# One more pass through TensorE's loop ahead of tile 0, and tile 0 turned and split by its own row blocks

## The reference

```
logits = z @ router_w + router_b            # 8 experts
top1   = argmax(softmax(logits))
h      = z @ w1[e] + b1[e]                  # 256 -> 2 x 1024
a, g   = split(h, 2)
y      = (a * sigmoid(g)) @ w2[e] + b2[e]   # 1024 -> 256, for the tokens with top1 == e
out    = x + y
```

## Time and profile before

| | us |
|---|---|
| median of 3 runs | 236.19 (235.63, 236.19, 237.41) |
| profiled execution | 235.62 |
| its span | 233.8 |
| TensorE busy in the span | 208.6 (89%) |
| DVE, ACT, POOL busy | 162.4, 123.8, 124.4 |
| mean granted TensorE clock | 0.947 of full |

### The profile page before, as it was taken

One profiled execution on the slowest core, in us unless ns is written; L12 is line 12 of the kernel. 1 busy time (PEld: TensorE's weight loads), 2 busy tenths in 40 slices (PEclk: granted clock), 3 DMA queues, 4 the chain that ended last, 5 costly groups with the idle time before them and its releaser, 6 DMA issues.

```text
span 233.8 us, 4272 instructions
## 1 busy us (share of the span) xinstructions
PE 208.6 (89%) x1505; PEld 196.2 (84%) x1507; DVE 162.4 (69%) x306; ACT 123.8 (53%) x204; POOL 124.4 (53%) x148
## 2 busy tenths in 40 slices
PE   7989858994799999999999999999999999999800
PEld 3858317994799999999999999999999999999700
DVE  5759935765902799389979969956995699559300
ACT  2457902453702858286785776738672757375000
POOL 5000177860800387438878778774877177018133
PEclk9999975999589999999999999999999999999985
DMA  5996338994491046956698597679268817101000
GB/s 153 358 354 251 158 85 247 266 352 145 112 294 45 24 162 135 293 183 206 154 329 226 182 313 129 219 204 292 77 215 215 265 49 239 32 1 57 1 24 10
DMA packets 31651, 41.25 MB, mean 176 GB/s; under 512 B 3208, under 2 KB 27913, under 8 KB 31498
## 3 DMA queue, kind: packets, MB, share of 16 engines
q1 hardware_dynamic: 26082, 28.32, 37.3%
q0 software_dynamic: 4608, 10.50, 18.8%
q10 hardware_dynamic: 936, 2.17, 2.4%
HBM read 36.78 MB, written 6.29 MB: 184 GB/s over the span
## 4 chain that ended last, share of the span: by engine, by line
PE 75%; DVE 10%; issue 8%; POOL 3%; ACT 2%; DVEq 0%; ACTq 0%; POOLq 0%
PE y_ps L967 8%; PE y_ps L969 8%; PE y_ps L968 8%; PE g_ps L941 7%; PE g_ps L946 6%; PE g_ps L942 6%; PE a_ps L946 6%; PE a_ps L942 6%; PE a_ps L941 6%; PE y_ps L829 4%; DVE arena L743 2%; POOL out_dram L375 2%; DVE u_lo L749 2%; PE a_ps L915 1%; DVE w_lo L641 1%
## 5 line engine op out<-in xcount | busy, mean ns | idle before, releaser
L375 POOL DMA_INDIRECT out_dram<-y_out,s_idx x32 | 45.6, 1424 | 54.9 <-DVE y_out L765 38.7
L491 ACT ACTIVATE arena<-g_ps,b_t 128x384 f32<-128x384 f32 (+1 forms) x64 | 34.5, 539 | 56.4 <-PE g_ps L946 56.4
L743 DVE SCALAR_TENSOR_TENSOR arena<-a_ps,b_t,arena 128x384 f32<-128x384 f32 (+1 forms) x64 | 36.2, 565 | 37.4 <-PE a_ps L946 35.8
L355 POOL DMA_INDIRECT xg<-x_rows,g_idx x32 | 37.7, 1177 | 40.5 <-DVE g_idx L705 24.6
L969 PE MATMUL y_ps<-w_hi,u_lo 128*128 128x256 f32 x168 | 48.6, 289 | 1.4 <-issue 1.4
L967 PE MATMUL y_ps<-w_hi,u_hi 128*128 128x256 f32 x168 | 49.7, 296 | 0.2
L968 PE MATMUL y_ps<-w_lo,u_hi 128*128 128x256 f32 x168 | 48.7, 290 | 0.0
L363 POOL DMA_INDIRECT y_out<-in_x_dram,g_idx x32 | 37.9, 1186 | 9.8 <-issue 9.8
L635 DVE TENSOR_TENSOR w_lo<-w_raw,w_hi 128x1024 fp32r<-128x1024 f32 x32 | 37.3, 1223 | 5.0 <-DMA xg<-x_rows,g_idx 3.7
L941 PE MATMUL g_ps<-xr_hi,w_hi 128*128 128x256 f32 (+3 forms) x128 | 37.7, 307 | 0.8 <-ACT xr_hi L479 0.6
L497 ACT ACTIVATE u_hi<-arena 128x384 fp32r<-128x384 f32 (+1 forms) x64 | 30.7, 480 | 14.3 <-DVE arena L743 14.2
(11 more groups left out here) (145 smaller groups left out, 305.0 us busy)
## 6 DMA issues: line engine op xcount, KB each, us to landing
w_raw<-in_L_ffn_w_dram SPq DMA_DIRECT2D x48, 512.0 KB, 7.5
arena<-in_x_dram SPq DMA_DIRECT2D x4, 512.0 KB, 5.9
x_rows<-arena ACTq DMA_DIRECT2D x4, 512.0 KB, 2.8
b_all<-in_L_ffn_b_dram SPq DMA_DIRECT2D x1, 1024.0 KB, 5.7
xg<-x_rows,g_idx POOLq DMA_INDIRECT x32, 6.5
y_out<-in_x_dram,g_idx POOLq DMA_INDIRECT x32, 4.4
out_dram<-y_out,s_idx POOLq DMA_INDIRECT x32
rb_rows<-in_L_ffn_router_b_dram ACTq DMA_DIRECT2D x4, 0.0 KB
```

What stands on the lines that cost most here:

```text
L355: nc.gpsimd.indirect_dma_start(out=xg[:, s * DIM:(s + 1) * DIM], out_offset=None, in_=x_rows, in_offset=bass.IndirectOffsetOnAxis(ap=g_idx ...
L375: nc.gpsimd.indirect_dma_start(out=out_flat, out_offset=bass.IndirectOffsetOnAxis(ap=s_idx[:, i * NSUB + s:i * NSUB + s + 1], axis=0), in_ ...
L743: V.scalar_tensor_tensor(dst, pair[c % RING][0][:, 0:n], b1_t[:, bass.ds(e * (2 * NC) + c, 1)], sig[:, c % SIG_RING, 0:n], ALU.add, ALU.mu ...
```

## The change

TensorE's loop counts one pass more. The sum of slots (L900), the keep-warm matmuls and the loads of the control words move into the loop, under `i == 1`. In pass 0 all conditions inside are false, so the pass computes nothing and only branches. Tile t is now pass t+1. In tile 0 only the row blocks that the size holds are turned, and ACT and DVE split only their columns, behind the branch on the number of blocks. Since fewer turnings no longer imply that all four gathers have landed, POOL waits for gathers 2 and 3 ahead of tile 1's gather. Branches for `SPLIT_C < NC`, which these sizes don't use, are dropped from `row_blocks` and `second_product`.

```diff
--- before.py
+++ after.py
@@ -387,6 +387,9 @@
             for i in range(NE):
                 if i + 1 < NE:
                     pool.wait_ge(xg_turned, (i + 1) * KH)
+                    if i == 0:
+                        for s in range(2, NSUB):
+                            pool.wait_ge(gathered[s], 16)
                     gather(i + 1)
                 if i > 0:
                     scatter(i - 1)
@@ -472,11 +475,11 @@
             if SPLIT_C:
                 w2_hi_part(0)
 
-            def split_x(i):
+            def split_x(i, n=ITEM):
 
                 for k in range(KH):
                     act.wait_ge(xg_turned, i * KH + (k + 1))
-                    nc.scalar.activation(xr_hi[:, k * ITEM:(k + 1) * ITEM], xk_ps[k][:, :], ACT.Copy)\
+                    nc.scalar.activation(xr_hi[:, k * ITEM:k * ITEM + n], xk_ps[k][:, 0:n], ACT.Copy)\
                         .then_inc(xr_hi_done[k], 1)
 
             def gates(i, e, c, n):
@@ -498,6 +501,8 @@
                     .then_inc(u_hi_done, 1)
 
             def gate_tile(i, e, n):
+                if i == 0:
+                    split_x(0, n)
                 for c in range(NC):
                     gates(i, e, c, n)
                     if 1 <= c <= SPLIT_C:
@@ -513,7 +518,6 @@
             last_tile = load_last(act)
             word_at = word_register(act, "word_at")
             load_word(act, word_at, 0)
-            split_x(0)
             for e in range(NE):
                 if_blocks(act, this_word(act, word_at), lambda blocks: gate_tile(e, e, blocks * P))
                 if e + 1 < NE:
@@ -724,12 +728,12 @@
             V.tensor_scalar(ctrl[:, 1 + NE:1 + TAB], owner, float(MORE), None, ALU.add)
             V.memset(ctrl[:, 1 + TAB:2 + TAB], 0).then_inc(ctrl_ready, 1)
 
-            def split_x(i):
+            def split_x(i, n=ITEM):
 
                 for k in range(KH):
-                    part_k = slice(k * ITEM, (k + 1) * ITEM)
+                    part_k = slice(k * ITEM, k * ITEM + n)
                     dve.wait_ge(xr_hi_done[k], i + 1)
-                    V.tensor_tensor(xr_lo[:, part_k], xk_ps[k][:, :], xr_hi[:, part_k].bitcast(F32), ALU.subtract)\
+                    V.tensor_tensor(xr_lo[:, part_k], xk_ps[k][:, 0:n], xr_hi[:, part_k].bitcast(F32), ALU.subtract)\
                         .then_inc(xr_lo_done[k], 1)
 
             def gated(i, e, c, n):
@@ -766,6 +770,11 @@
 
             def gate_tile(i, e, blocks):
                 n = blocks * P
+                if i == 0:
+                    split_x(0, n)
+                    w1_lo_part(0, 3)
+                    w2_lo_part(0)
+                    dve.wait_ge(b2_loaded, 16)
                 for c in range(NC):
                     gated(i, e, c, n)
                     if 1 <= c <= SPLIT_C:
@@ -795,11 +804,6 @@
             last_tile = load_last(dve)
             word_at = word_register(dve, "word_at")
             load_word(dve, word_at, 0)
-            split_x(0)
-            w1_lo_part(0, 3)
-            if SPLIT_C:
-                w2_lo_part(0)
-            dve.wait_ge(b2_loaded, 16)
             for e in range(NE):
                 if_blocks(dve, this_word(dve, word_at), lambda blocks: gate_tile(e, e, blocks))
                 if e + 1 < NE:
@@ -893,34 +897,40 @@
             for b in range(3, NB // 2):
                 rotate_blocks(b)
 
-            pe.wait_ge(b1_t_done, 1)
-            pe.wait_ge(q_oh_ready, 1)
-            for n in range(NB):
-                pe.wait_ge(slots_ready, n + 1)
-                last = T.matmul(early_ps[:, 0:TS], slot_oh[:, n, :], q_oh[:, n * TS:(n + 1) * TS],
-                                start=(n == 0), stop=(n == NB - 1))
-            last.then_inc(idx_summed, 1)
-            keep_warm(late_ps, 16)
-
-            pe.wait_ge(ctrl_ready, 1)
-            last_tile = load_last(pe)
-            next_word = pe.alloc_register("next_word")
-            pe.reg_load(next_word, ctrl[0:1, 1:2])
-
-            def turn(i16):
-
-                for s in range(NSUB):
+            next_reg = pe.alloc_register("next_reg")
+            last_reg = pe.alloc_register("last_reg")
+            pe.reg_mov(next_reg, 0)
+            pe.reg_mov(last_reg, NE - 1)
+
+            def sum_slots():
+
+                pe.wait_ge(b1_t_done, 1)
+                pe.wait_ge(q_oh_ready, 1)
+                for n in range(NB):
+                    pe.wait_ge(slots_ready, n + 1)
+                    last = T.matmul(early_ps[:, 0:TS], slot_oh[:, n, :], q_oh[:, n * TS:(n + 1) * TS],
+                                    start=(n == 0), stop=(n == NB - 1))
+                last.then_inc(idx_summed, 1)
+                keep_warm(late_ps, 16)
+
+                pe.wait_ge(ctrl_ready, 1)
+                pe.reg_load(last_reg, ctrl[0:1, 0:1])
+                pe.reg_load(next_reg, ctrl[0:1, 1:2])
+
+            def turn(i16, blocks):
+
+                for s in range(blocks):
                     pe.wait_ge(gathered[s], i16)
                     for k in range(KH):
                         last = T.transpose(xk_ps[k][:, s * P:(s + 1) * P], xg[:, s * DIM + k * P:s * DIM + (k + 1) * P],
                                            ident[:, :])
-                        if s == NSUB - 1:
+                        if s == blocks - 1:
                             last.then_inc(xg_turned, 1)
 
             def first_product(i, size, at1, at16):
                 n = SIZES[size]
-                with pe.If(((i - 1) & 15) >= NE - 1):
-                    turn(at16)
+                with pe.If(((i - 2) & 15) >= NE - 1):
+                    turn(at16, BLOCKS[size])
                 for c in range(NC):
                     if c % CPU1 == 0:
                         pe.wait_ge(w1_split[c // CPU1], at1)
@@ -947,42 +957,33 @@
                                             start=False, stop=(k == KH - 1))
                         last.then_inc((a_done, g_done)[ag], 1)
 
-            def row_blocks(subs, at1, at2, at16, end=False):
+            def row_blocks(subs, at1, end=False):
 
                 for c in range(NC):
-                    if c < SPLIT_C:
-                        pe.wait_ge(u_lo_done[c], at1)
-                    else:
-                        if c == SPLIT_C or c % CPU2 == 0:
-                            pe.wait_ge(w2_loaded[c // CPU2], at16)
-                        pe.wait_ge(pair_free[c], at2 if c >= CARRIED else at1)
+                    pe.wait_ge(u_lo_done[c], at1)
                     wv = slice(c * DIM, (c + 1) * DIM)
                     for s in subs:
-                        at = (c if c < SPLIT_C else c - SPLIT_C) * ITEM + s * P
+                        at = c * ITEM + s * P
                         uv = slice(at, at + P)
                         dst = y_ps[s // 2][:, (s % 2) * DIM:(s % 2 + 1) * DIM]
                         first = c == 0 and s == subs[0]
                         final = c == NC - 1 and s == subs[-1]
-                        if c < SPLIT_C:
-                            T.matmul(dst, u_hi[:, uv], w2_hi[:, wv], start=first, stop=False)
-                            T.matmul(dst, u_hi[:, uv], w2_lo[:, wv], start=False, stop=False)
-                            last = T.matmul(dst, u_lo[:, uv], w2_hi[:, wv], start=False, stop=final)
-                        else:
-                            last = T.matmul(dst, u_nat[:, uv], w2_raw[:, wv], start=first, stop=final)
+                        T.matmul(dst, u_hi[:, uv], w2_hi[:, wv], start=first, stop=False)
+                        T.matmul(dst, u_hi[:, uv], w2_lo[:, wv], start=False, stop=False)
+                        last = T.matmul(dst, u_lo[:, uv], w2_hi[:, wv], start=False, stop=final)
                 if end:
                     last.then_inc(mm2_done, 1)
 
-            def second_product(word, at1, at2, at16):
-
-                if SPLIT_C:
-                    pe.wait_ge(w2_split, at1)
+            def second_product(word, at1):
+
+                pe.wait_ge(w2_split, at1)
                 for h in range(2):
                     pe.wait_ge(y_done[h], at1)
                 with pe.If(f_size(word) >= BLOCKS.index(4)):
-                    row_blocks((3,), at1, at2, at16)
+                    row_blocks((3,), at1)
                 with pe.If(f_size(word) >= BLOCKS.index(3)):
-                    row_blocks((2,), at1, at2, at16)
-                row_blocks((0, 1), at1, at2, at16, end=True)
+                    row_blocks((2,), at1)
+                row_blocks((0, 1), at1, end=True)
 
             def by_size(word, low, high, body):
 
@@ -995,19 +996,23 @@
                 with pe.Else():
                     by_size(word, middle, high, body)
 
-            with pe.Fori(0, TAB) as i:
-                with pe.If(i <= last_tile):
-                    word = pe.snap(next_word, min_val=0, max_val=127)
-                    at1 = pe.to_reg(i + 1)
-                    at2 = pe.to_reg(i + 2)
-                    at16 = pe.to_reg(i * 16 + 16)
-                    next16 = pe.to_reg(i * 16 + 32)
```

(21 more changed lines are left out.)

## The result

The changed kernel takes **241.44 us** (median of 4 runs, 240.09 to 241.98) against 236.34 of the kernel before (4 runs): ratio 1.0203, 95% interval 1.0143 to 1.0263. It is slower by 2%, and the forecast was 232.5. The profiled execution took 241.87, with a span of 240.1 (233.8 before). Some executions, of v_large_first and x_narrow further down above all, took over 1.5% longer than their kernel's fastest, and the ratios leave such executions out.

What follows compares the result with a forecast made beforehand. TensorE, 89% busy, was taken as bound by code-fetch gaps and halved clock. Entry +3.3, tile 0 to tile 1 -7.0, later tiles nothing: -3.7 from 235.62 gives 231.9, or 232.5 on the median's footing; range 229.0 to 236.5.

Steps and rivals of the forecast that it cites:

- With both there, the stretch 54.08 to 70.91, 16.83 us, becomes: Tile 0's first product to tile 1: with both code pieces fetched, 9.8 us, saving 7.0 (4.4 gaps, 2.6 clock).
- the fetched code does not last: Rival, 8%: code fetched in pass 0 is pushed out before tile 0's second turning, both gaps return; 239.5 us.
- Only 2 cache lines!: Skill's rule on TensorE's code store: the change would end at 239.5, with code packets every tile; trace judged against it.
- At least those seven seem to live together: TensorE's code store: seven packets arrived, the loop's jump back caused no gap or later packet, so seven pieces fit together.
- Pass 0 mis-sized: Ahead of the sum of slots: two fetches, 3.0 and 2.7 us, bring L900's start to 29.3; sum ends 3.5 later.
- The upper bound of L900: Sum of slots, sixteen L900 back to back: at most 3.4 us at half clock; 1.5, the lower bound, was taken.
- the entry: Up to tile 0's first product: +3.5 for pass 0, +0.3 keep-warm, -0.5 narrower tile, together +3.3 us.
- later tiles nothing: Tiles after tile 1: no change, since their code is there and all they wait for moves along.
- Tile 0 by its own blocks: Tile 0's turning and split: two of eight transposes go, -0.43, and ACT's copy narrows, -0.1; together -0.5 us.
- The clock: After tile 0's first product: granted clock 1.00 without the gaps, worth 2.6 of the 7.0 us saved.
- two fetches in pass 0: Sign: two code packets between 23 and 28 us, with a gap of 5 to 6 us ahead of L911.
- the fetch of tile 0's own code: Ahead of tile 0's turning: the fetch at 32.36 stays, since pass 0 does not go there; gap of 3.2.

Runs made afterwards that it cites:

- e1_narrow: The kernel before with only tile 0 turned and split by its own row blocks and POOL waiting for gathers 2 and 3; 233.17 us, ratio 0.9858.
- e2_no_pass0: The changed kernel with TensorE's loop counted from 1, so that pass 0 alone is gone; 236.08 us, ratio 0.9992 to the kernel before.
- e4_narrow_padded: The kernel before with tile 0 by its own blocks, plus 26 never-run instructions ahead of the loop (compiled program grows by 27); 236.52 us, ratio 1.0021.
- e3_three_tests: The kernel before with three always-true tests added at the head of TensorE's loop; 241.49 us, ratio 1.0213.

## Why the fetched code is lost

**e5_walk**: the change with a chain of tests in place of the branch tree, so that pass 0 steps through every copy in ascending order before it comes to the turning.

```diff
+                    for size in range(len(SIZES)):
+                        with pe.If(f_size(pe.snap(next_reg, min_val=0, max_val=127)) == size):
+                            first_product(i, size, at1, at16)
```

> The changed kernel with the branch tree replaced by a chain of six tests, so that pass 0 steps through the code of all first products in ascending order and then the turning's and the second product's. Theory A (a fetched piece goes into the place behind the piece being run, so pieces fetched out of order are overwritten when those between are filled in): fetched in order they all stay; L911 starts 14 to 20 us later than in the kernel before, but no gap is left at tile 0: neither ahead of its turning nor ahead of the second product, and no packet of TensorE's code after pass 0. Theory B (TensorE keeps at most seven pieces and drops the oldest): gaps come back at tile 0. Total about 250 in A, 255 to 258 in B, since six tests a tile also cost in the head.

Measured: 247.76, ratio 1.0489 (1.0443 to 1.0535), where theory A had about 250. It takes long, since TensorE stands still for 19 us in pass 0, but it tells the two theories apart:

```profile
42.49 0.74 PE L911 MATMUL y_ps<-q_oh,work 128*128 128x44 f16 x16 [19.06 <-issue]
...
67.10 0.46 PE L956 MATMUL a_ps<-xr_lo,w_hi 128*128 128x320 f32 x2
67.40 0.27 PE L925 MATMUL a_ps<-ident,xg 128*128 128x128 f32 x1
...
78.67 0.40 PE L951 MATMUL g_ps<-xr_hi,w_hi 128*128 128x352 f32 x1 [1.45 <-issue]
67.40:78.67 11.27, 9.83 (x82) 9.51 (x80) 7.86 (x10) 5.59 (x8) 5.58 (x4) 1.00 0.84 241
q8 instruction: 7, 0.11, 0.2%
```

The last two lines are the window from the second turning to tile 1, and the code queue over the whole run. The second turning follows the first product with no gap at all, and in the window from 43 us to the end the queue q8 moved nothing. From 67.40 to 78.67 are 11.3 us, less 1.45 for the longer head 9.8: what the prediction had for this stretch with the code in place, and the granted clock there is 1.00, as it had too. Theory A forecast this; theory B (seven pieces, oldest dropped) fails. So does any rule that goes by the number of pieces alone, since this kernel runs through the same loop's code as the changed one.

**s3_before and s3_after**: the two kernels with three sizes (256, 384, 512).

```diff
-    SIZES = (256, 288, 320, 352, 384, 512)
+    SIZES = (256, 384, 512)
```

> The kernel before with three sizes (256, 384, 512) in place of six, so that TensorE's loop has three copies of the first product and is some 640 instructions shorter; tiles of 257 to 352 rows are computed 384 wide. Theory (code comes piece by piece, the next piece is asked for on entering one, only a jump past it stands still): tile 0's copy, the turning and the second product now lie in neighbouring pieces, so no gap ahead of tile 0's turning nor ahead of the second one, 3 us or more each in the kernel before. Rival (the gaps belong to the turning or to the branches themselves): they stay. The time is longer by the wider tiles, near 240 either way, and tells nothing.

> The changed kernel with the same three sizes. The loop then needs only some six pieces of code, two or three of them fetched in pass 0. Theory A (pieces fetched ahead of their turn are overwritten once those between are filled in): packets for the turning's and the second product's pieces come twice, in pass 0 and again during tile 0: 7 to 8 packets in all. Theory B (TensorE drops the oldest when more than seven are there): six pieces fit, each is fetched once, 5 to 6 packets in all.

Measured, one execution each: 239.86 and 244.63, wider tiles and so no comparison with the others. In s3_before five packets, and no gap ahead of the second turning; ahead of the first TensorE waits for the gathers alone. In s3_after eight (whole run of each):

```profile
q8 instruction: 5, 0.08, 0.1%
```

```profile
q8 instruction: 8, 0.13, 0.2%
```

s3_before's second turning, for comparison with the 3.03 of the earlier trace rows:

```profile
55.61 0.51 PE L946 MATMUL a_ps<-xr_lo,w_hi 128*128 128x384 f32 x2
55.96 0.27 PE L915 MATMUL a_ps<-ident,xg 128*128 128x128 f32 x1
```

Pass 0 adds three packets again, though s3_before's code came in five where the kernel before keeps seven. That cannot be want of room. Here the repeated packets cost no gap: TensorE goes from the first product (57.48) to the second turning (57.83) without one, so only their number tells. What the changed kernel and s3_after share is that pass 0 jumps over pieces not yet fetched.

**v_large_first**: e1_narrow with the copies in the order 512, 384, 352, 320, 288, 256, so that tile 0 skips the code of tile 1.

```diff
-                with pe.If(f_size(word) < middle):
-                    by_size(word, low, middle - 1, body)
+                with pe.If(f_size(word) >= middle):
+                    by_size(word, middle, high, body)
```

> e1_narrow with the copies of the first product in the order 512, 384, 352, 320, 288, 256. Tile 0 (320) then jumps over the code of tile 1's size (352), which it did not skip before. Theory A: the gap ahead of tile 0's turning and the one after its first product stay at 3 to 4 us, and the piece skipped comes out of order: at tile 1 a gap of about 3 us and new packets, then again the turning's code once more, 2 to 6 us slower than e1_narrow: 235 to 239. Theory B (order does not matter, eight pieces fit): one gap of 3 us at tile 1 and none after it, 10 or fewer packets, 235 to 237.

Measured: 245.65 to 256.55 in 4 runs, its profiled execution and two more between 254 and 257, so it is told without a ratio. The trace is of the execution of 254.12. Fourteen packets, and gaps not only at tile 1 but at the next tile of that size, 117 us later:

```profile
74.22 0.63 PE L945 MATMUL g_ps<-xr_hi,w_hi 128*128 128x352 f32 x1 [5.92 <-issue]
...
191.53 0.64 PE L945 MATMUL g_ps<-xr_hi,w_hi 128*128 128x352 f32 x1 [6.92 <-issue]
q8 instruction: 14, 0.23, 0.4%
```

Code that had run at tile 1 was gone at the other. Theory B allowed ten packets at most. Theory A had the direction right and was too mild by far: it said 2 to 6 us over e1_narrow's 233.17, and even the fastest of the four executions is 12.5 over it.

## Looking for a better version

**v_five_sizes** leaves the size 384 out of e1_narrow, **v_four_sizes** 288 and 384.

```diff
-    SIZES = (256, 288, 320, 352, 384, 512)
+    SIZES = (256, 288, 320, 352, 512)      # v_five_sizes
+    SIZES = (256, 320, 352, 512)           # v_four_sizes
```

> e1_narrow without the size 384, which no tile of these inputs has: one copy of the first product less between tile 0's copy and the turning. Theory: the piece with the turning is asked for when tile 0's copy enters its last piece, about 2 us ahead of need, so of the 3.7 us gap ahead of the second turning 1 or less is left, and the next piece costs up to 2.4 at the start of the second product; the clock may still fall. 0 to 3 us faster than e1_narrow: 230 to 233. Rival (the gap is not a matter of distance): 233.

> e1_narrow with sizes 256, 320, 352, 512. Two tiles of 288 become 320 wide: 2 x 96 matmuls x 32 columns, +2.6 us at full clock. Theory: tile 0's copy, then the turning, then the second product lie in neighbouring pieces; the gap ahead of tile 0's turning shrinks to the wait for the gathers (-0.5 to -1), the 3.7 us gap ahead of the second turning goes with its halved clock (-4 to -6), a gap of up to 2.4 stays at the start of the second product. Net 229.5 to 233. Rival (only the sum of gaps moves about): 234 to 236.

Measured: 234.58, ratio 0.9941 (0.9906 to 0.9977), and 234.83, ratio 0.9947 (0.9914 to 0.9981), 10 runs each. Both forecasts missed (230 to 233 and 229.5 to 233); v_four_sizes came out where its rival had it. Both beat the kernel before and neither e1_narrow's ratio. In v_five_sizes the gap was only split in two, 1.26 + 2.57 in place of 3.74:

```profile
54.03 0.30 PE L919 MATMUL a_ps<-ident,xg 128*128 128x128 f32 x1 [1.26 <-issue]
...
57.67 0.38 PE L971 MATMUL y_ps<-w_hi,u_hi 128*128 128x256 f32 x1 [2.57 <-issue]
```

In v_four_sizes it did not shrink (4.72 us), only the gap ahead of the first turning went. I take it that my count of where pieces end was off and the turning lay in the next one; no run shows it.

**x_second_first** puts the second product's code ahead of the first products; **x_narrow** adds e1_narrow's edits to it.

```diff
+                    with pe.If(i >= 1):
+                        ...                                   # turning, second product of tile i-1
+                    with pe.If(i <= last_tile):
+                        ...                                   # first product of tile i
```

> The kernel before with the loop's code in another order: the turning and the second product of the tile before stand ahead of the first products, the order of execution is the same. Theory A: the code for them is there early, but the loop's end now lies behind all six copies, so after tile 0's first product TensorE stands about 3 us for that piece, and later tiles meet pieces out of order: 8 or more packets, no gain. Rival (a piece once fetched stays, eight fit): one gap of 3 us after tile 0's first product, nothing in later tiles, 7 or 8 packets, 1 to 2 us faster than before.

> x_second_first and e1_narrow together: the second product's code ahead of the first products, tile 0 by its own blocks. x_second_first showed an entry gap of 8.0 us (two pieces, one after the other) and 2.1 in place of 3.0 + 1.4 later, all seven pieces fetched in ascending order and none twice. Theory: this one also asks for its pieces in order, so no gap after tile 0; the narrower tile gives 0.5 to 0.8: 232.5 to 233.5, ratio 0.983 to 0.99. Rival (the shift of the code by some 30 instructions moves a boundary into tile 0 or makes a piece come out of order): 235 or more, with a gap at a later tile.

Measured: x_second_first 233.6 in its one execution, below the lowest of 19 of the kernel before (234.21). That is what its rival had, 7 packets and one gap after tile 0's first product (2.08), and not theory A's "no gain" with 8 packets or more. As I read its seven packets, nothing was fetched twice, as when all pieces are met in ascending order, so the miss would be in how I applied theory A. The run alone does not tell that from the rival, a piece once fetched stays; the changed kernel and s3_after speak against the rival. The entry gap grew to 8.01, two pieces as I read it. x_narrow was inconclusive in time, 1.0018 (0.9909 to 1.0128); its trace has nine packets and a gap of 1.48 ahead of the turning that follows tile 1's first product, which fits pieces out of order, as its rival had it. The best version measured with an interval stays e1_narrow.

## Why the prediction was wrong

- **The step that failed** is "With both there, the stretch 54.08 to 70.91, 16.83 us, becomes", with its sum of 9.8: 15.85 were measured, with a gap of 4.03 in it. The 9.8 was right for code in place (e5_walk), that the code would still be there was not. So -1.0 stands where the forecast had -7.0. The rival "the fetched code does not last" had this, at 8%, with 239.5; the 1.9 beyond it are of the size of what the later tiles' heads add. Its mechanism is right, its condition was not: it "decides at the number of pieces that TensorE keeps", and s3_after shows the packets coming twice with room to spare. Nor is "Only 2 cache lines!" (the Trainium skill, "Advanced Engine Details and Errata", ISA Cache) the cause, and this case's trace does not agree with it: in e5_walk no code packet came after 43 us.
- The evidence that misled me: in the kernel before, every piece happens to be met in ascending order. "At least those seven seem to live together" was true for that order alone. I took a store's size from a trace in which the rule by which it replaces pieces could not show.
- **Pass 0 mis-sized**: 3.5 us forecast for the end of the sum of slots, 5.0 measured; 29.3 for the first L911, 31.56 measured. I priced a fetch by the idling it left (3.0 and 2.7). In pass 0 two packets cost 7.72, 3.9 each; the third starts at 31.1 and takes 0.88 us, too late for the L911 at 31.56 to have waited for it. Counted in the same way, e5_walk's 19.06 hold five, 3.8 each: the sixth starts at 42.1 and takes 0.98, and L911 starts at 42.49.
- **The upper bound of L900 was not needed**: the sixteen took 0.74 us, under my lower bound of 1.5. This miss hid part of the one before, and so did others: by the first product's start the entry had cost +3.6 against +3.3 forecast. That near agreement is luck.
- **"later tiles nothing" failed**: from tile 1's first matmul to the end of the span are 165.9 us, 162.9 before, +3.0. The waits at seven heads make 3.2 of idling, of which 0.50 lies ahead of that matmul; e2_no_pass0, with the same loop, has 2.3. I costed the work of every moved matmul and no branch in the loop. The diff shows two tests more on a tile's way to its copy, for `i == 1` and `i >= 1`, with their arithmetic.
- **Tile 0 by its own blocks**: -0.5 forecast, -0.76 at the first product's start. As a whole the edit was worth -3.0, which went when the code was padded to its old length (e4_narrow_padded).
- **The clock** was forecast at 1.00 behind the first product. It was 0.86 over 62.38 to 74.20, where the kernel before has 0.75 over 57.11 to 70.91: with the gap still there it did not reach the full clock, and e5_walk, without the gap, did.
- Right: two fetches in pass 0, the fetch of tile 0's own code left ahead of its turning, and no harm seen from POOL's, DVE's or ACT's new order.

What is shown is that the order in which pieces are met decides, and not their number (the change against e5_walk, s3_after against s3_before). What stays open is how TensorE places its pieces. That one is overwritten when the pieces skipped come in is the reading that fits the change, e5_walk, s3_after and the direction of v_large_first; that pieces are given up at the jump back would fit the first three too. No run shows the place itself, and which code a packet holds is inferred from when it comes. Open too is why the fetch ahead of the second turning starts 0.2 us after TensorE falls idle in the kernel before and 1.0 after in the change.

## What to carry to other kernels

A loop with branches has a layout: draw which pieces of code a run meets, in which order, before paying for one ahead of time; code fetched over a piece not yet met may have to be fetched again. Give each test in a loop's head a price, since it can be on the path of the engine that it feeds. And when an edit gains more than its work is worth, pad the code to its old length before believing it.

## What the runs showed of the hardware that I had not expected

- Tests with their arithmetic at the head of TensorE's loop show as idling: 0.66 us a head for three (e3_three_tests, 4.6 in 7).
- Twenty-seven instructions that never run cost 3.35 us (e4_narrow_padded against e1_narrow, medians), and a gap of 1.23 us came back inside tile 0's second product.
- A piece of code costs TensorE 3.8 to 3.9 us where several are wanted one after the other (19.06 for five in e5_walk, 7.72 for two in the change). Code that had run at one tile had to be waited for again 117 us later (v_large_first), while in e5_walk nothing was fetched again after seven packets.
- With the gaps gone, the stretch from the second turning to tile 1 ran at a granted 1.00 (e5_walk), 0.75 in the kernel before.
